# Where the LoRA layer's block sums are made: on GpSimd during attention's first group, or in the preamble through DRAM

## What is computed

```python
xn = layernorm(x)
# attention: 128 heads, head dim 4, latent 64, rope dim 64
c_q, c_kv = xn @ Wq_down, xn @ Wkv_down
q_c, k_c, v_c = c_q @ Wq_up, c_kv @ Wk_up, c_kv @ Wv_up
q_r, k_r = xn @ Wq_rope, xn @ Wk_rope
scores = (q_c . k_c + q_r . k_r) / sqrt(68)
s = (softmax(scores) @ v_c) @ Wo
# feed forward: weights are one quarter, tiled four times, plus a rank 2 term
def qlora(x, wq, A, B):
    return x @ tile(wq, (1, 4)).T + (x @ A.T @ B.T) / 2
g = silu(qlora(silu(qlora(xn, w1q, a1, b1)) * qlora(xn, w3q, a3, b3), w2q, a2, b2))
out = x + s * g
```

## Time and profile before

| what | value |
|---|---|
| median of 3 runs | 2003.47 us (2002.44 to 2006.35) |
| the profiled execution, its time | 2006.13 us |
| the profiled execution, span from first to last instruction | 2004.3 us |
| PE busy | 1949.5 us, 97% of the span |
| DVE busy | 1404.0 us, 70% |
| ACT busy | 1052.0 us, 52% |
| POOL busy | 491.7 us, 25% |
| preamble | 0 to some 76 us |
| attention's first group | some 77 to 192 us |
| other groups of attention | to some 1796 us |
| chain that ended last: PE / DVE / ACT | 91% / 3% / 1% of the span |

### The profile page before, as it was taken

How to read it: one execution, slowest core, us unless ns; L and a number is a source line. 1 busy time by engine, 2 the same in 40 slices (tenths; PEclk the granted TensorE clock), 3 DMA queues, 4 the chain that set the end, 5 groups by cost and what they waited for, 6 DMA issues and landing times.

```text
span 2004.3 us, 38494 instructions
## 1 busy us (share of the span) xinstructions
PE 1949.5 (97%) x12448; PEld 1500.9 (75%) x12448; DVE 1404.0 (70%) x1654; ACT 1052.0 (52%) x1535; POOL 491.7 (25%) x798
## 2 busy tenths in 40 slices
PE   7799999999999999999999999999999999997998
PEld 5577777777777777777777777777777777764776
DVE  7788676767676777767676767676777767775644
ACT  5455555555555555555555555555555555553222
POOL 2345222221212121212121222212221212111221
PEclk9999999999999999999999999999999999998999
DMA  7411112121212121211111111212121211224331
GB/s 256 158 24 39 39 38 40 33 45 26 49 28 50 25 49 29 49 28 42 34 38 39 35 39 33 45 26 49 28 50 26 48 29 39 62 59 129 105 101 52
DMA packets 131723, 105.87 MB, mean 53 GB/s; under 512 B 52222, under 2 KB 96302, under 8 KB 131614
## 3 DMA queue, kind: packets, MB, share of 16 engines
q1 hardware_dynamic: 131678, 105.29, 22.3%
HBM read 51.76 MB, written 26.21 MB: 39 GB/s over the span
## 4 chain that ended last, share of the span: by engine, by line
PE 91%; DVE 3%; ACT 1%; issue 1%; SPq 0%; DMA 0%; POOLq 0%; POOL 0%; DVEq 0%; ACTq 0%
PE pj L890 34%; PE st L860 23%; PE sx L877 12%; PE ob L837 12%; PE ap L1474 2%; PE sx L845 1%; PE yp L1507 1%; PE zp L1507 1%; DVE mx L796 1%; PE gp L1428 1%; PE zp L1460 1%; PE gp L1440 0%; DVE slot L810 0%; DVE slot L806 0%; PE gp L1429 0%
## 5 line engine op out<-in xcount | busy, mean ns | idle before, releaser
L796 DVE TENSOR_REDUCE mx<-sx 128x4 f32<-128x1024 f32 x512 | 626.8, 1224 | 427.7 <-PE sx L877 409.9
L777 ACT ACTIVATE probs<-st 128x1024 f32<-128x1024 f32 x512 | 512.7, 1026 | 172.8 <-PE st L860 172.8
L747 ACT ACTIVATE slot<-pj 64x512 fp32r<-64x512 f32 x512 | 304.0, 594 | 432.9 <-PE pj L890 426.5
L697 POOL CAST k<-kc 64x512 fp32r<-64x512 f32 x256 | 168.0, 657 | 1031.0 <-PE st L860 1031.0
L860 PE MATMUL st<-slot,k 89*128 89x512 f32 x1024 | 417.8, 408 | 2.6 <-DMA slot<-mrow 1.4
L860 PE MATMUL st<-slot,krlh 128*128 128x512 f32 x1024 | 407.0, 397 | 0.0
L890 PE MATMUL pj<-xh,wh 128*128 128x512 f32 x1024 | 402.0, 393 | 4.2 <-PEq L202 3.1
L890 PE MATMUL pj<-xh,wl 128*128 128x512 f32 x1024 | 401.9, 392 | 0.0
L890 PE MATMUL pj<-xl,wh 128*128 128x512 f32 x1024 | 401.6, 392 | 0.0
L806 DVE TENSOR_TENSOR slot<-pj,slot 64x512 fp32r<-64x512 f32 x512 | 352.7, 689 | 16.3 <-ACT slot L747 0.3
L877 PEld LDWEIGHTS sx<-k,slot 88*128 88x128 f32 x2048 | 306.4, 190 | 72.0 <-issue 29.2
(11 more groups left out here) (172 smaller groups left out, 1323.7 us busy)
## 6 DMA issues: line engine op xcount, KB each, us to landing
w_stage<-in_Wq_rope SPq DMA_DIRECT2D x64, 256.0 KB, 3.0
c_scratch<-stage SPq DMA_DIRECT2D x32, 256.0 KB, 3.0
c_in<-c_scratch SPq DMA_DIRECT2D x128, 64.0 KB, 1.9
o_scratch<-o_sb SPq DMA_DIRECT2D x128, 64.0 KB, 2.1
k<-kc SPq DMA_DIRECT2D x128, 48.0 KB
slot<-kc SPq DMA_DIRECT2D x256, 24.0 KB
k<-kx SPq DMA_DIRECT2D x128, 48.0 KB
slot<-kx SPq DMA_DIRECT2D x256, 24.0 KB
```

Source lines behind the costliest of these rows:

```text
L697: nc.gpsimd.tensor_copy(k1[0:64, s, :, :].rearrange("p a n -> p (a n)"), krh[:, bp * CH:(bp + 1) * CH]).then_inc(k_ready, 1)
L747: nc.scalar.activation(slot1[0:64, (k - 1) % NS, e, :, :], pj[64 * e:64 * e + 64, :].rearrange("p (a n) -> p a n", a=2), ACT.Copy).then_in ...
L777: nc.scalar.activation(probs[:, k % NS, kt], st[:, kt], ACT.Exp, scale=SCALE).then_inc(exp_done, 1)
L796: nc.vector.tensor_reduce(mx[:, p, lo:lo + 4], sx[:, :, :].rearrange("p a (b k) -> p (a b) k", b=2), axis=AX.X, op=ALU.max).then_inc(red_d ...
```

## The change

- `blocks_summed(c)` on POOL in the preamble adds the four column blocks of the normalised, token-major rows `xn` of a chunk: three additions of 128 x (4 x 128) elements into `xs_sum`. It waits for the chunk's rows (`xn_ready`) and for the transposes of the sum before (`ev_done`). It stands ahead of the first rope weight, behind the first, behind the second, and behind the latent copies.
- `xn` has two buffers, by the chunk's parity; a chunk's rows wait for the transposes and the sums of the chunk two before.
- NE is 13: the thirteenth tile of a chunk (n = 12) holds four PE transposes of `xs_sum` in an `ev` bank. ACT copies it to `stage`, SP stores it in the new `s_dram`. `bank(u)` says which tile used a bank last.
- In attention's first group `sync_head` on SP first waits for all stored tiles (step 3) and loads a chunk of `s_dram` into `s_raw` behind the steps 3, 6, 9 and 12. `pool_head` with its 28 additions is gone. `sh` is made behind steps 5, 8, 11, 14 and `sl` behind 6, 9, 12, 15 (before: 5, 9, 13, 15 and 6, 11, 14, 15).
- The masks `mk` are made on DVE at the start of the preamble, ahead of the statistics of chunk 0, and no longer behind step 2 of the first group.

The diff, cut to its core:

```diff
-NE = 12
+NE = 13
...
+    s_dram = nc.dram_tensor("s_scratch", [128, T], F32, kind="Internal").ap()
...
-        xn = sb(ctx, "xn", [128, NTL, D])
+        xn = [xn_even, sb(ctx, "xn_odd", [128, NTL, D])]
+        xs_sum = sb(ctx, "xs_sum", [128, NTL, 128])
...
+        def bank(u):
+
+            return u % NE % 4
...
+                    elif n == NE - 1:
+                        sp.dma_start(s_dram[:, c * CH:(c + 1) * CH], tile).then_inc(stored[(c * NE + n) % NST], 16)
...
         @block.gpsimd
         def _(pool):
+            def blocks_summed(c):
+                pool.wait_ge(xn_ready, (c + 1) * NTL)
+                wait(pool, ev_done, c * NE)
+                for k in range(1, KD):
+                    if k > 1:
+                        pool.wait_ge(xs_step, 3 * c + k - 1)
+                    before = xs_sum[:, :, :] if k > 1 else xn[c % 2][:, :, 0:128]
+                    nc.gpsimd.tensor_tensor(xs_sum[:, :, :], before, xn[c % 2][:, :, 128 * k:128 * k + 128],
+                                            ALU.add).then_inc(xs_step, 1)
...
             pool.wait_ge(up_lo, 5)
+            blocks_summed(0)
             for s in range(NS):
                 pool.wait_ge(w_staged[s % 2], 16 * (s // 2 + 1))
                 nc.gpsimd.tensor_copy(wh[:, s], w_stage[:, s % 2]).then_inc(w_hi, 1)
                 pool.wait_ge(w_hi, s + 1)
                 nc.gpsimd.tensor_tensor(wl[:, s], w_stage[:, s % 2], wh[:, s], ALU.subtract).then_inc(w_ready, 1)
+                if s in (0, 1):
+                    blocks_summed(s + 1)
...
             pool.wait_ge(ct_copy, 2)
+            blocks_summed(NC - 1)
+            pool.wait_ge(xs_step, 3 * NC)
...
             def normalise(c):
                 for i in range(NTL):
                     n = c * NTL + i
-                    wait(dve, transposed, (c - 1) * NTL + i + 1)
-                    nc.vector.tensor_scalar(xn[:, i, :], x_in[:, n, :], mv[:, n, 0:1], rs[:, 3, n:n + 1],
+                    wait(dve, transposed, (c - 2) * NTL + i + 1)
+                    if i == 0:
+                        wait(dve, xs_step, 3 * (c - 1))
+                    nc.vector.tensor_scalar(xn[c % 2][:, i, :], x_in[:, n, :], mv[:, n, 0:1], rs[:, 3, n:n + 1],
                                             ALU.subtract, ALU.mult).then_inc(xn_ready, 1)
...
+            dve.wait_ge(ident_ready, 1)
+            for n, (lo, hi, scale) in enumerate(((8, 12, 1.0), (4, 8, 0.5), (4, 6, 1.0), (2, 4, 0.5))):
...
+            dve.wait_ge(m_step, 12)
             statistics(0)
             normalise(0)
...
                 if u >= 4:
-                    wait_tile(pe, u - 4)
+                    wait_tile(pe, max(v for v in range(u) if bank(v) == bank(u)))
...
+                elif n == NE - 1:
+                    pe.wait_ge(xs_step, 3 * (c + 1))
+                    for i in range(NTL):
+                        last = nc.tensor.transpose(ev[n % 4][:, 128 * i:128 * i + 128], xs_sum[:, i, :], ident[:, :])
+                    last.then_inc(ev_done, 1)
...
+    def sync_head(sp, k):
+        if k == 3:
+            tiles_stored(sp, stored, range(NC * NE))
+        if k in (3, 6, 9, 12):
+            c = k // 3 - 1
+            cs = slice(c * CH, (c + 1) * CH)
+            sp.dma_start(s_raw[:, cs], s_dram[:, cs]).then_inc(s_loaded, 16)
...
-    def pool_head(pool, k):
-        if k == 1:
-            tiles_stored(pool, stored, range(NC * NE))
-        if 1 <= k < 15:
-            for n in (2 * k - 2, 2 * k - 1):
-                c, n = n // 7, n % 7
-                cs = slice(c * CH, (c + 1) * CH)
-                terms = [xx[:, kt, cs] for kt in range(KD) for xx in (xh, xl)]
-                if n:
-                    pool.wait_ge(s_step, 7 * c + n)
-                nc.gpsimd.tensor_tensor(s_raw[:, cs], s_raw[:, cs] if n else terms[0], terms[n + 1],
-                                        ALU.add).then_inc(s_step, 1)
...
-        if k in (5, 9, 13, 15):
-            c = (5, 9, 13, 15).index(k)
-            act.wait_ge(s_step, 7 * c + 7)
+        if k in (5, 8, 11, 14):
+            c = k // 3 - 1
+            act.wait_ge(s_loaded, 16 * c + 16)
...
     def vector_head(dve, k):
-        if k == 2:
-            for n, (lo, hi, scale) in enumerate(((8, 12, 1.0), (4, 8, 0.5), (4, 6, 1.0), (2, 4, 0.5))):
...
-            dve.wait_ge(m_step, 12)
...
-        if k in (6, 11, 14, 15):
-            c = (6, 11, 14, 15).index(k)
+        if k in (6, 9, 12, 15):
+            c = k // 3 - 2
```

More of the change, by code:

```diff
@@ L134, in attn_ffn_layer @@
         lora_raw, = region(nc, AT_KX, ("lora_raw", [64, T], F32))
+        mk, = region(nc, AT_P + 8 * T, ("mk", [128, 8], F32))
+        xn_even, = region(nc, AT_KX + 4 * T, ("xn_even", [128, CH // 128, D], F32))
         room = ExitStack()
@@ L155, in attn_ffn_layer @@
                               ct_copy)
-        ends = finish(nc, sb, at_sems, passed, sem, x_tok, xh, xl, parts[5], lora_raw, ident, stored, o_dram, r_dram, wo, w1qT, b1T, w3qT,
+        ends = finish(nc, sb, at_sems, passed, sem, x_tok, xh, xl, parts[5], lora_raw, mk, ident, stored, s_dram, o_dram, r_dram, wo, w1qT, b1T, w3qT,
                       b3T, w2qT, a2T, b2T, out_tok)
@@ L188, in _, with project_inputs @@
             rest(pe)
-def project_inputs(nc, sb, sem, passed, x_tok, wq_down, wkv_down, wk_rope, a1T, a3T, wv_up, wq_up, wk_up, v_dram, c_dram,
+def project_inputs(nc, sb, sem, passed, x_tok, wq_down, wkv_down, wk_rope, a1T, a3T, wv_up, wq_up, wk_up, v_dram, c_dram, s_dram,
                    xh, xl, kc, krlh, c_in, ident, w_stage, wh, wl, wq_rope, w_staged, w_hi, w_ready, probs, stage,
-                   stored, c_loaded, ct_hi, ct_lo, ct_copy, lora_raw):
+                   stored, c_loaded, ct_hi, ct_lo, ct_copy, lora_raw, mk, xn_even):
     NTL = CH // 128
@@ L239, in project_inputs @@
         xn_ready = sem("xn_ready")
+        xs_step = sem("xs_step")
+        m_step = sem("mask_step")
         transposed = sem("transposed")
@@ L467, in chunk @@
                     statistics(c + 2)
+            dve.wait_ge(ident_ready, 1)
+            for n, (lo, hi, scale) in enumerate(((8, 12, 1.0), (4, 8, 0.5), (4, 6, 1.0), (2, 4, 0.5))):
+                nc.vector.tensor_reduce(mk[:, 2 * n:2 * n + 1],
+                                        ident[:, :].rearrange("p (j c) -> p j c", j=4)[:, :, lo:hi],
+                                        axis=AX.XY, op=ALU.add).then_inc(m_step, 1)
+                dve.wait_ge(m_step, 3 * n + 1)
+                nc.vector.tensor_scalar(mk[:, 2 * n + 1:2 * n + 2], mk[:, 2 * n:2 * n + 1], -2.0, 1.0,
+                                        ALU.mult, ALU.add).then_inc(m_step, 1)
+                dve.wait_ge(m_step, 3 * n + 2)
+                nc.vector.tensor_scalar(mk[:, 2 * n:2 * n + 1], mk[:, 2 * n:2 * n + 1], scale, None,
+                                        ALU.mult).then_inc(m_step, 1)
+            dve.wait_ge(m_step, 12)
             statistics(0)
@@ L646, in load_v @@
                 if at.first:
-                    tiles_stored(sp, stored, range(NE * bp + 8, NE * bp + NE))
+                    tiles_stored(sp, stored, range(NE * bp + 8, NE * bp + 12))
                 sp.dma_start(v_it[:, bp % 2, :, :],
@@ L939, in finish @@
     den, num = region(nc, AT_W + 4096, ("den", [128, KD, CH], F32), ("num", [128, KD, CH], F32))
-    s_raw, sh, mk = region(nc, AT_P, ("s_raw", [128, T], F32), ("sh", [128, T], F32R), ("mk", [128, 8], F32))
+    s_raw, sh = region(nc, AT_P, ("s_raw", [128, T], F32), ("sh", [128, T], F32R))
     sl, = region(nc, AT_P, ("sl", [128, T], F32R))
@@ L964, in finish @@
         ap = [banks.enter_context(nc.psum_tensor(f"ap{i}", [128, D], F32)) for i in range(2)]
-    masks = sem("masks")
-    m_step = sem("mask_step")
     lora_hi_done = sem("lora_hi_done")
@@ L976, in finish @@
     b_done = sem("b_done")
-    s_step = sem("s_step")
+    s_loaded = sem("s_loaded")
     sh_done = sem("sh_done")
@@ L1280, in vector_head @@
     def vector_head(dve, k):
-        if k == 2:
-            for n, (lo, hi, scale) in enumerate(((8, 12, 1.0), (4, 8, 0.5), (4, 6, 1.0), (2, 4, 0.5))):
-                nc.vector.tensor_reduce(mk[:, 2 * n:2 * n + 1],
-                                        ident[:, :].rearrange("p (j c) -> p j c", j=4)[:, :, lo:hi],
-                                        axis=AX.XY, op=ALU.add).then_inc(m_step, 1)
-                dve.wait_ge(m_step, 3 * n + 1)
-                nc.vector.tensor_scalar(mk[:, 2 * n + 1:2 * n + 2], mk[:, 2 * n:2 * n + 1], -2.0, 1.0,
-                                        ALU.mult, ALU.add).then_inc(m_step, 1)
-                dve.wait_ge(m_step, 3 * n + 2)
-                nc.vector.tensor_scalar(mk[:, 2 * n:2 * n + 1], mk[:, 2 * n:2 * n + 1], scale, None,
-                                        ALU.mult).then_inc(m_step, 1)
-            dve.wait_ge(m_step, 12)
         if k in (4, 7, 10, 13):
@@ L1521, in nothing @@
         pass
```

(2 more changed lines are left out.)

8 lines of the change are left out of this document (4 added, 4 removed).

## The result

| | runs | median us | lowest to highest | ratio to before, 95% interval |
|---|---|---|---|---|
| before, same chip | 20 | 2004.53 | 1999.38 to 2007.60 | |
| changed | 20 | 2008.09 | 2005.49 to 2011.81 | 1.0019 [1.0013, 1.0026] |
| before, second comparison | 15 | 2001.99 | 1998.87 to 2005.11 | |
| changed, second comparison | 8 | 2007.38 | 2006.42 to 2011.34 | 1.0030 [1.0019, 1.0041] |

The change cost 0.2 to 0.3%, 4 to 6 us. The first comparison lies just inside the 0.2% that I called no change, the second just outside. The forecast was +0.9 us. The profiled execution of the changed kernel took 2011.81 us (span 2010.0), its slowest; a second trace of the same kernel has a span of 2004.6.

The account below looks back on a forecast made before the run. The prediction took PE to bound the later groups, with some 15 us open in the first; 7.7 us gained there against 8.6 lost in the preamble gave +0.9, 2004.4 us at the median, range 1998.0 to 2010.0.

Parts of the forecast that it names:

- Chunk 0's contention: Preamble, chunk 0: POOL's additions delay DVE's last row of chunk 1 by 1.5 us, between 0 and 2.8.
- the 1.6 us given back: Preamble, chunk 2: weights no longer run beside the four normalised rows, which returns about 1.6 us.
- rival two: Preamble: the clock falls behind PE's idle ahead of chunks 1 and 2, up to 1.7 us each; 2007.8, chance 0.14.
- (a): First group: without masks and POOL's addition beside L790, the reduction behind the row scores starts 2.1 us earlier.
- (b): First group: with the 3.41 us wait cut to 1.3, the clock stays up; 1.7 us, between 0 and 1.7.
- (c): First group: PE's waits for DVE at 118.39 and 134.97 go, 0.7 us each.
- (d): First group: PE's wait at 162.06 goes because DVE's copy ends 3.1 us earlier; all 2.0 us gained.
- (e): First group: half of PE's 0.90 us wait for POOL at 192.27 goes; 0.5 us, between 0 and 0.9.
- One: Preamble: the additions hardly hold DVE up, so the cost is about 2.5 us; 1998.3 at the median, chance 0.18.
- Three: First group: gives back only the safe 4.5 us, as the next wait replaces the one removed; 2007.6, chance 0.10.
- Four: First group: `s_raw` from DRAM is late at `sh`, blocking ACT's order; given no time of its own.
- the prediction's last sign: Later groups or behind attention: any change there would mean that the working misses something.

Follow-up runs that it names:

- e7: The changed kernel with 8 and 12 overwritten matmuls on PE ahead of the first tiles of chunks 1 and 2; ratio to before 1.0012.
- e1: The changed kernel without its twelve preamble additions, the thirteenth tile transposing xn's first block alone; 1997.56 us, ratio to before 0.9967.
- e3: The changed kernel, complete, with the preamble additions moved to other times and two xs_sum buffers; 1998.86 us, ratio to before 0.9973.
- e4: The changed kernel's preamble without the masks, with the old first group (28 POOL additions, masks behind step 2); 2014.02 us, ratio to before 1.0056.
- e2: The kernel before with the masks alone moved ahead of the statistics, additions in place; ratio to before 0.9986.
- e9: The kernel before, run again unchanged for a second trace; ratio to before 1.0003.
- e8: The kernel e3 with twelve matmuls whose result nobody reads at the end of PE's preamble; ratio to before 0.9991.
- e5: The kernel before without the additions of attention's first group, old preamble, masks still behind step 2; ratio to before 0.9982.

## Why the prediction held in its two halves and was 3 to 5 us low

**The preamble: 8.6 predicted, 8.6 and 8.5 measured, but not term by term, and in part by luck.** The central step, that DVE's chain is through when POOL is, held to 0.02 us for chunk 1 and for chunk 2 (57.77 against 57.75). Chunk 0's contention (1.5) was met: the third set of transposes is at 29.49 for 28.02, in the second pair at 30.00 for 28.36. Three terms are off:

- Chunk 1's first tile came 4.1 us later (4.2 in the second pair), where chunk 0 and chunk 1 were to give 2.1 + 3.0 = 5.1. The transposes of 0.63 are counted twice: they were put into chunk 0 and lie inside chunk 1's wait too, as the prediction itself says. The last 0.2 to 0.4 are small differences.
- Chunk 2's first tile was to come another 4.4 us later (the 1.6 us given back lie behind it), 9.5 in all. It is 8.0 us late in the first pair and 6.5 in the second. With the clock kept up (e7) the term is 16.5 - 14.2 = 2.3 in place of 4.4. Both weights were to hold up DVE's chain; it was through behind the first of them, and the second ran beside `cs` (58.52 to 59.93, POOL 58.03 to 60.31), which took its usual 0.68 and 0.69 us.
- Behind chunk 2's first tile the sum has -1.6 + 0.7 = -0.9 us; with the clock up it is 25.4 - 24.8 = +0.6.

At full clock this makes 4.1 + 2.3 + 0.6 = 7.0 us. The fall of the clock, which the sum left out and gave to rival two, added 1.6 in one trace and 1.4 in the other. So terms that were 1.6 us too high (0.6 of it the transposes counted twice) and a clock cost that was put at nothing met at 8.6. By e1 the thirteenth tile costs 0.2 to 0.5 us, less than its 0.63 and 0.7.

**The first group: 7.7 predicted, 6.2 and 7.4 measured.** (a) was met as a wait and not as time. The wait fell from 3.41 to 1.32, 2.1 us, but the stretch that holds it, from the projection ahead of it to the maxima, became only 0.6 and 0.7 us shorter: 6.86 and 6.88 in the two traces of before, 6.30 and 6.18 in those of the change. The stretch before, in the changed kernel, and in e3 (columns as in e7):

```profile
90.75:97.61 6.86, 3.45 (x16) 2.77 (x16) 6.42 (x17) 1.19 (x2) 6.41 (x5) 1.00 0.00 0
100.73:107.03 6.30, 4.98 (x17) 3.89 (x17) 4.00 (x5) 1.19 (x2) 1.13 (x2) 0.74 0.00 0
91.84:96.64 4.80, 3.48 (x16) 2.77 (x17) 3.74 (x5) 1.19 (x2) 0.96 (x1) 1.00 0.00 0
```

DVE was done earlier, but in the changed kernel PE ran the projections there at a granted clock of 0.74 (0.76 in the second trace), which used up the gain; e3, with the same group at 1.00, has the whole 2.1. This is also why e4's wait is 1.94: with masks and additions its stretch takes 6.85 us, as before, and PE at 0.77 fills more of it. So a wait shrinks when the waiting engine itself gets slower, and its size need not be the time that its removal gives.

(b), 1.7 us of clock, was no gain to count on. The clock is at 1.00 where 0.57 was, but has fallen elsewhere: the share lost to it in the first 32 us of the group (1 less the granted clock, times 8 us, over four stretches) is 4.4 and 6.9 us in the two traces of before, 5.1 and 3.2 in those of the change. (c) was met: both waits of 0.7 are gone, and they stay in e2, as the additions do. (d), the 2.0 us, was called safe and is not: the second trace of before has no such wait and is as long. One row of one execution was taken for a property of the kernel. (e), put at 0.5, was the whole 0.9: the wait on POOL at 192.27 is gone in both traces of the change, and the kernels with the additions have it (0.95 in e9, 0.95 in e2, 0.99 in e4). Counted roughly, by the waits and the share lost to the clock, the first pair gives 2.1 - 0.7 + 1.4 + 2.0 + 0.9 = 5.7 us against 6.2, the second 2.1 + 3.7 + 1.5 + 0 + 0.9 = 8.2 against 7.4. So in each pair one of (b) and (d) failed and the other paid, which is luck.

**The rivals.** One (little contention) is out by e1 and e4. Two came true in its mechanism (a granted clock under 1 in chunks 1 and 2 was its sign), at waits of 2.1 and 2.8 us, below the 3 from which it was to decide, and at 1.4 to 1.6 us an execution in place of up to 3.4 (e7). Three is out: no wait took the place of the removed ones, and the group gave over 4.5. Four made no wait that the traces show: the one that names ACT's exponentials has 0.90 us in the changed kernel, and 0.90 and 0.91 in the two traces of before.

**The rest of the +4 to +6 us.** The marks show +2.4 and +1.2 at step 22. The rest of each comparison, 1.4 us in the first and 4.8 in the second, is not explained; it is what the prediction's last sign warned of, a part that the working misses. In the other kernels the time by the ratio differs from the mark at step 22 too, from 1 us less (e1) to some 5 us more (e4, e8), so the difference does not belong to this change alone. In the later groups PE never waits but once (1.3 us; before, 1.3 and 1.4), and the length of this stage runs from 1528.8 (e2) to 1534.5 (e3, among the fastest) over all traces, whatever the kernel. It differs by 4.9 us between the two traces of before, so single traces can't place so little.

The rule of the Trainium skill (SBUF — State Buffer, Who interferes with whom), that the second engine is blocked until the first instruction ends, agrees with the chain ahead of chunk 1: no instruction there lost more than one of POOL's; the longest took 1.12 us beside one of 1.27. The copy between the slots is at odds with it: it took 3.81, 2.53 and 3.10 us at most in the traces of before, e9 and e4, all with additions beside it, in place of 0.69, a delay of 3.1, 1.8 and 2.4 us, each more than one addition of 1.3; a copy by POOL ran there too, ahead of the additions.

## What to carry to other kernels

Moving work to an idle engine is not free when its instructions hold up those of the engine that feeds PE: here twelve additions on POOL, with the weights pushed behind them, cost 8 us beside DVE's chain of short instructions and nothing where they stood 6 us later (chunk 0) or 4 to 12 us earlier (the other chunks). Before work is moved, look for the stretch in which the neighbour is idle or does what a trace shows undisturbed, and give the work its own buffer so that it can stand there. Read a wait in two traces of the same kernel before it goes into a sum as certain, and price it by the distance between two marks around it, with the granted clock beside it. When a sum comes out right, compare its terms too: here errors of some 1.6 us in opposite directions cancelled.

## What the runs showed of the hardware that was not expected

- The twelve mask instructions with one element per partition took 0.15 to 0.17 us each, with additions running on POOL (e9: 1.89 us from 96.16) and without (e5: 1.89 us from 94.24). Instructions of 4 elements per partition took up to 1.12, but not the reciprocal among them: it took 0.18 with an addition running (37.39). The statistics, which read 512 elements per partition from SBUF, were not held up either: 0.695 us at most over the sixteen of e3, four of which ran beside additions (31.89 to 34.35, POOL 31.87 to 34.53).
- The granted clock fell behind idle times of 2.1 and 2.8 us in one trace and behind only the second in another, of the same kernel; a fall cost 1.4 to 1.6 us where PE was what others waited for (e7), and a stretch at 0.73 cost nothing where PE waited for others anyway (e8).
- With PE busy throughout, the same 1530 us of work took up to 0.4% more or less from one trace to another (1528.8 to 1534.5; in the two traces of before 1528.8 and 1533.7), at a granted clock of 1.00 over the whole stretch.
